# A hybrid of scan, linear attention and routed attention: image passes whose step and input rows are copied by DMA from SBUF rows

## The chip, the cores and the metric
The kernel runs on one core of one Trainium2 chip. The metric is device time in microseconds of one launch. All work is in float32, but for the three bfloat16 parts into which the kernel before splits the scan's rows.

## The reference, cut to what matters
The input is four images of 16 x 16 places with 192 channels. One layer follows another:

```
x = x + conv_scan(group_norm(x))     # per image: in_proj to 96 + 96, 3x3 depthwise conv, silu,
                                     # 4 selective scans over 256 places, layer norm, gate, out_proj
t = t + performer(layer_norm(t))     # 12 heads of 16, 64 features: relu(.) + 0.001
t = t + ffn_attn(layer_norm(t))      # router picks 6 of 12 heads, softmax attention, layer norm
# one scan direction k (rows, columns, and both backwards), 96 channels, 16 states per channel:
d = softplus(dt_proj(x_dbl) + b);  h = h * exp(d * A) + (d * u) * B;  y = sum_n h * C
```

A scan has 96 x 16 = 1,536 independent recurrences for each image and direction, each 256 places long. `exp(d*A)` is called the decay, `d*u` the input, `(d*u)*B` the drive.

## The kernel before, in words
**Units.** The scans are done in units of 128 partitions x 512 elements. A unit holds 8 channels x 16 states on its partitions and two images of 256 places side by side in its row. There are 2 halves of two images x 4 directions = 8 scans, each of 12 units, so 96 units. Backward directions use inputs that GpSimd has laid out in reverse (`orders`, L516 to L530).

**One unit.** The step `d` and the input `d*u` are made once for each scan on 96 partitions, one for each channel (`step2`, L976 to L997). A unit needs each channel row on 16 partitions. The row is split into bfloat16 parts hi, mid and lo (ScalarE L720 and L724, GpSimd L544 and L549), which DMAs on SyncE's queue stack above one another (L446), and TensorE spreads them with a 0/1 matrix into PSUM: `step_bc` (L1384) and `inp_bc` (L1388), each with two banks. ScalarE makes the decay from `step_bc` (L732, `decay`). VectorE multiplies `inp_bc` by the rows of B (L1010) and runs the recurrence (L1019, `state`). GpSimd multiplies `state` by the rows of C (L559, `outp`), and TensorE sums the 16 states with a 0/1 band into `y_acc` (L1397), a float32 matmul that shows as two. The rows of B and C lie on 32 partitions in `bc`, and eight DMAs each copy 16 of these partitions to the 128 partitions of `b_rep` and `c_rep` (L433).

**Order.** Each engine has one instruction stream, written out by hand: a loop over 96 units, and after it the list `rest`. Semaphores join the streams. Between two units stand items from the planner `side_work`: the making of the next scan's rows (`preparing`, with fixed places such as PRE_RAW and PRE_INP), the second half's convolution, the transposes of weights, and from unit 52 on the attention and feed-forward steps of images 0 and 1 (`ATTN_STEPS`, `FFN_STEPS`), one or two steps a unit. Images 2 and 3 can start only when unit 95 is done, because a scan holds two images. The planner, run on its own constants, leaves 91 steps in `rest`: the end of image 0 from its second head step (`t0`), image 1 from `hT`, and all of images 2 and 3. A step's vector part stands in `side` of each engine: VectorE adds the 0.001 and takes the maximum for the queries (L1161) and the keys (L1166), and applies the norms (L1062).

**SyncE's queue** holds all DMAs in one order: the loads, then for each scan eight copies of B, eight of C, and nine of the stack.

Of the kernel before, what the change touches and what calls it, by code (L numbers as in the profile page):

```python
# [24 lines left out]
P = 128  # L25
IMAGES, SIDE, CH = 4, 16, 192
L = SIDE * SIDE
HALVES = 2
IMG = IMAGES // HALVES
TOK = IMG * L  # L30
TILES = TOK // P
CK = CH // 2
DI, NS, RANK, DIRS = 96, 16, 12, 4
GRP = P // NS
UNITS = DI // GRP
CHUNK = 32
CHUNKS = DI // CHUNK
PER_CHUNK = CHUNK // GRP
# [7 lines left out]
RING = 3  # L46
SLOTS = 3
STATE_SLOTS = 4
Y_LAG = 3
# [6 lines left out]
PRE_RAW, PRE_CLIP, PRE_EXP, PRE_SERIES, PRE_LN = -4, -3, -2, -1, -1  # L56
PRE_MAX, PRE_MAX_SERIES, PRE_INP = 0, 1, 2

PRE_HI, PRE_REST, PRE_MID, PRE_LO = (2, 3), (4, 5), (5, 6), (6, 6)
SECOND_LATER = 3  # L60
LOG_MAX = 82.0

CONST2 = 3 + 1 + HPC + TOPK
ONES = 13
BEHIND = (0, 0, 0, 6)
FIRST_STEP = 4
ADD_Y = 3
Z_GATED = 2
ACC_ROWS = IMG * (SIDE + 2) - 2
SCANS = HALVES * DIRS  # L70
# [6 lines left out]
HEAD_STEPS = ["s0", "t0", "s1", "w0", "t1", "w1"]  # L77
# [9 lines left out]
FRONT_BESIDE = ((1, "xh"), (9, "conv0"), (11, "conv1"), (13, "conv2"), (17, "silu"), (21, "z"))  # L87
WEIGHTS_FIRST = 14

UNITS_AFTER = {step: 1 for step in ("q0", "q1", "q2", "kv00", "kv01", "kv10", "wqk", "wv", "fq", "fk")}  # L90
# [4 lines left out]
def side_work():  # L95

    beside = [[] for _ in range(SLOT_COUNT)]

    for at, step in FRONT_BESIDE:
        beside[at].append((step, 1))  # L100
    for i, step in enumerate(WEIGHT_STEPS):
        beside[WEIGHTS_FIRST + 2 * i].append((step, 0))
# [3 lines left out]
    done, ready = [0, 0], [DIRS * UNITS + FIRST_STEP, DIRS * UNITS + FIRST_STEP + 1]  # L106
    for u in range(DIRS * UNITS, SLOT_COUNT):
        held = 0.0
        for n in (0, 1):
            if ready[n] > u or done[n] >= (len(steps) if n == 0 else done[0]):  # L110
                continue
            step = steps[done[n]]
            if step in HEAD_STEPS and (n % IMG or step == "w0"):
# [8 lines left out]
    at = {step: i for i, step in enumerate(steps)}  # L122
    done += [0, 0]
    rest = []
    while min(done) < len(steps):
        for n in range(IMAGES):
            if done[n] == len(steps) or (n and done[n - 1] < min(len(steps), done[n] + 1 + BEHIND[n])):
                continue
            if n >= IMG and (done[n] == at["tT"] and done[n - IMG] <= at["fv"] or done[n] == at["un"] and done[n - IMG] <= at["fo"]):
                continue  # L130
            rest.append((steps[done[n]], n))
            done[n] += 1
# [3 lines left out]
def products(step, n):  # L136
# [7 lines left out]
    if step in HEAD_STEPS:  # L144
        heads = range(int(step[1]), TOPK, 2)
        return {"s": [f"s{n}{j}" for j in heads], "t": [f"pt{n}{j}" for j in heads], "w": [f"pv{n}", f"pd{n}"] * (step == "w0")}[step[0]]
# [3 lines left out]
def preparing(u, at):  # L150

    n = (u - at) // UNITS + 1
    if u == max(0, at + SECOND_LATER - (at > PRE_INP)):
# [4 lines left out]
def ring_plan():  # L158

    beside, rest = side_work()  # L160
    names = ["w_in", "gm0", "w_xp", "w_dt", "gv0", "w_alog", "xh0_0", "xh1_0", "w_fold", "gm1", "z_0", "gv1", "d0"]
# [9 lines left out]
    for i, name in enumerate(names):  # L171
        if name[:2] in ("pv", "pd"):
            at = FINAL_RING - 2 + (name[1] == "d")
        else:
            at = turn % (RING if i < early else FINAL_RING - 2)
            turn = turn + 1 if i + 1 != early else 0
# [5 lines left out]
def hybrid_kernel(nc, x, in_proj_w, conv_w, conv_b, x_proj_w, dt_w, dt_b, A_logs, Ds, norm_g, norm_b, out_proj_w,  # L182
# [5 lines left out]
    with ExitStack() as ctx:  # L188
# [31 lines left out]

        step_bc = [ctx.enter_context(nc.psum_tensor(f"step_bc{i}", [P, TOK], F32)) for i in range(2)]
        inp_bc = [ctx.enter_context(nc.psum_tensor(f"inp_bc{i}", [P, TOK], F32)) for i in range(2)]
        y_acc = ctx.enter_context(nc.psum_tensor("y_acc", [P, TOK], F32))
        banks = [ctx.enter_context(nc.psum_tensor(f"ring{i}", [P, TOK], F32)) for i in range(RING)]
        banks += step_bc + inp_bc + [y_acc]

        def bank(name):
# [3 lines left out]
        x_tok = sb("x_tok", [P, HALVES * TILES, CH])  # L231
# [11 lines left out]
        band = sb("band", [P, 2 * DI - GRP])  # L243
        spread = sb("spread", [DI, PER_CHUNK, P], BF16)
# [17 lines left out]
            "room_b", [([CK, 2, HALVES * TOK], F32), ([FEAT, HPC, FEAT], F32), ([FEAT, HPC, HD], F32), ([CK, HPC, FEAT], F32)],  # L262
            [([P, PAIRS, TOK], F32)])
        valr = sb("valr", [1, IMG, 3 * HEADS, HD])
        acc, opw, hn = shared("room_e", [([DI, ACC_ROWS, SIDE], F32), ([CK, 2, DI], F32)], [([P, TILES, CH], F32)])
# [19 lines left out]
        xpad, wsel1 = shared("room_w", [([DI, IMG, SIDE + 2, SIDE + 2], F32)], [([CK + 1, 2, 3, CK], F32)])  # L285
# [1369 lines left out]
```

## Time and profile before

| | us |
|---|---|
| median of 3 runs (lowest, highest) | 463.25 (460.02, 463.73) |
| profiled execution: its own time | 463.01 |
| its span, first to last instruction | 461.3 |
| busy of the span: TensorE matmul, VectorE, ScalarE, GpSimd | 371.3, 346.4, 179.8, 206.9 |
| moved by DMA | 12.69 MB |

The profile is of one execution. Busy time of an engine counts its compute instructions alone. PE is TensorE's matmul, PEld its weight load, DVE VectorE, ACT ScalarE, POOL GpSimd, SPq SyncE's queue. The granted clock is TensorE's, as a share of full speed. The DMA share is the mean busy share of the core's 16 DMA engines. In a row, "idle before" is time in which the engine had nothing running just before such an instruction, and the name behind it is what ended that time.

### The profile page before, as it was taken

The numbers are of one execution on the slowest core, as the hardware profiler recorded it, in microseconds if no ns is written. First come the engines' busy times: TensorE is split into PE (matmuls) and PEld (weight loads), VectorE is DVE, ScalarE is ACT, GpSimd is POOL, SyncE is SP. The second block draws the span as 40 slices with busy tenths as digits, with TensorE's granted clock in tenths as the row PEclk, the third lists the DMA queues.
The fourth block names the chain that finished last, engine by engine and source line by source line (L and its number), as shares of the span: only waits on it lengthen the run. The fifth ranks groups of instructions, "written<-read, shape, count | busy, mean of one in ns | idle before, by whom it ended". The sixth has DMA issues, their size and how long they took to land. (4 is left out here: it accounts for less than half of the span.)

```text
span 461.3 us, 5553 instructions
## 1 busy us (share of the span) xinstructions
PE 371.3 (80%) x1669; PEld 214.3 (46%) x1669; DVE 346.4 (75%) x622; ACT 179.8 (39%) x405; POOL 206.9 (45%) x210
## 2 busy tenths in 40 slices
PE   5825499697887867857999998896989999969691
PEld 4612133142332312323557555553865786958450
DVE  5885989878999999999789898987457356263514
ACT  2565354554563534423243332335225211135340
POOL 7131697867895967774653863451121010000001
PEclk9999889979897987785999999999799989588966
DMA  5502212011121110110101010000000000000000
GB/s 121 106 21 64 56 26 64 23 41 34 23 58 34 47 40 18 40 43 9 47 21 33 11 34 1 0 2 1 2 17 1 1 0 17 2 1 1 1 17 18
DMA packets 15743, 12.69 MB, mean 28 GB/s; under 512 B 7279, under 2 KB 11361, under 8 KB 15713
## 3 DMA queue, kind: packets, MB, share of 16 engines
q1 hardware_dynamic: 15713, 12.33, 11.7%
q8 instruction: 14, 0.23, 0.2%
q14 instruction: 16, 0.13, 0.1%
HBM read 2.62 MB, written 0.79 MB: 7 GB/s over the span
## 5 line engine op out<-in xcount | busy, mean ns | idle before, releaser
L559 POOL TENSOR_TENSOR outp<-state,c_rep 128x512 f32<-128x512 f32 x96 | 126.4, 1321 | 93.0 <-PE y_acc L1397 43.1
L1019 DVE TENSOR_TENSOR_SCAN state<-decay,inp_bc 128x512 f32<-128x512 f32 x96 | 117.2, 1221 | 9.3 <-DVE inp_bc L1010 4.3
L1397 PE MATMUL y_acc<-outp,band 128*96 128x512 f32 x192 | 111.2, 666 | 6.7 <-DVE y_sum L1034 2.6
L732 ACT ACTIVATE decay<-step_bc,a_neg 128x510 f32<-128x510 f32 x96 | 64.9, 683 | 47.0 <-PE step_bc L1384 46.8
L1010 DVE TENSOR_TENSOR inp_bc<-b_rep,inp_bc 128x512 f32<-128x512 f32 x96 | 65.5, 682 | 7.1 <-PE inp_bc L1388 6.9
L1388 PE MATMUL inp_bc<-room_s,spread 96*128 96x512 bf16 x96 | 41.0, 427 | 31.1 <-DVE state L1019 31.0
L494 POOL TENSOR_TENSOR rs<-mv,neg_half 128x2 f32<-128x2 f32 x16 | 11.1, 696 | 120.0 <-DVE mv L1055 119.9
L1384 PE MATMUL step_bc<-room_s,spread 96*128 96x512 bf16 x96 | 39.9, 415 | 12.7 <-DMA room_s<-lo 11.6
L1397 PEld LDWEIGHTS y_acc<-outp,band 128*96 128x96 f32 x192 | 34.3, 182 | 24.7 <-issue 10.3
L1388 PEld LDWEIGHTS inp_bc<-room_s,spread 96*128 96x128 bf16 x96 | 9.9, 103 | 65.9 <-DVE state L1019 56.8
L1384 PEld LDWEIGHTS step_bc<-room_s,spread 96*128 96x128 bf16 x96 | 10.4, 109 | 32.5 <-issue 27.3
L720 ACT CAST hi<-step 96x512 bf16<-96x512 f32 x16 | 9.9, 616 | 33.4 <-DVE step L989 24.7
L1507 PE MATMUL ring<-kvw,tT 96*128 96x480 f32 (+1 forms) x48 | 21.2, 567 | 0.0
L1132 DVE RECIPROCAL spl<-y_acc 96x256 f32<-96x256 f32 x4 | 7.0, 1754 | 15.4 <-PE y_acc L1436 15.4
L1125 DVE TENSOR_REDUCE nmax<-ring 128x2 f32<-128x512 f32 x19 | 12.0, 680 | 7.1 <-PE step_bc L1407 3.9
L1501 PE MATMUL ring<-tT,qw 96*128 96x256 f32 (+1 forms) x64 | 16.6, 404 | 0.8 <-issue 0.8
L544 POOL TENSOR_TENSOR step<-step,hi 96x512 f32<-96x512 f32 x14 | 16.1, 1151 | 0.0
L549 POOL TENSOR_TENSOR lo<-step,mid 96x512 bf16<-96x512 f32 x14 | 15.9, 1154 | 0.0
L1501 PEld LDWEIGHTS ring<-tT,qw 96*128 96x128 f32 (+1 forms) x64 | 12.8, 202 | 5.9 <-issue 4.3
L724 ACT CAST mid<-step 96x512 bf16<-96x512 f32 x16 | 9.9, 616 | 13.6 <-POOL step L544 13.4
L1525 PEld LDWEIGHTS ring<-cbd,room_b 128*128 128x128 f32 x96 | 13.7, 227 | 1.0 <-issue 1.0
L1525 PE MATMUL ring<-cbd,room_b 128*128 128x34 f32 x96 | 13.6, 307 | 0.0
(346 smaller groups left out, 650.8 us busy)
## 6 DMA issues: line engine op xcount, KB each, us to landing
b_rep<-bc SPq DMA_DIRECT2D x64, 32.0 KB, 1.9
c_rep<-bc SPq DMA_DIRECT2D x64, 32.0 KB, 2.0
room_s<-hi SPq DMA_DIRECT2D x24, 64.0 KB, 2.0
room_s<-mid SPq DMA_DIRECT2D x24, 64.0 KB, 2.0
room_s<-lo SPq DMA_DIRECT2D x24, 64.0 KB, 2.0
x_tok<-in_x_dram SPq DMA_DIRECT2D x2, 384.0 KB, 3.8
out_dram<-room_g SPq DMA_DIRECT2D x4, 192.0 KB, 2.0
room_a<-in_L_attn_w_qkv_dram SPq DMA_DIRECT2D x1, 432.0 KB, 6.5
```

Source lines behind the costliest of these rows:

```text
L544: g.tensor_tensor(step2[:, i, :], step2[:, i, :], hi[:, i, :], ALU.subtract).then_inc(S["rest"], 1)
L549: g.tensor_tensor(lo[:, i, :], step2[:, i, :], mid[:, i, :], ALU.subtract).then_inc(S["lo"], 1)
L559: g.tensor_tensor(outp[:, u % SLOTS, :], state[:, u % STATE_SLOTS, :], c_rep[:, n % 2, :], ALU.mult).then_inc(S["outp"], 1)
L732: a.activation(decay[:, u % SLOTS, :, 1:L], step_bc[u % 2][:, :].rearrange("p (b l) -> p b l", b=IMG)[:, :, 1:L], ACT.Exp, scale=a_neg[:, ...
L1010: v.tensor_tensor(inp_bc[u % 2][:, :], b_rep[:, n % 2, :], inp_bc[u % 2][:, :], ALU.mult).then_inc(S["drive"], 1)
L1019: v.tensor_tensor_scan(state[:, u % STATE_SLOTS, :], decay[:, u % SLOTS, :, :].rearrange("p b l -> p (b l)"), inp_bc[u % 2][:, :], 0.0, AL ...
L1384: t_.matmul(step_bc[u % 2][:, :], spread[:, q, :], stack[:, n % 2, j, 0:TOK], start=True, stop=True).then_inc(S["bc_step"], 1)
L1388: t_.matmul(inp_bc[u % 2][:, :], spread[:, q, :], stack[:, n % 2, j, TOK:2 * TOK], start=True, stop=True).then_inc(S["bc_inp"], 1)
L1397: t_.matmul(y_acc[0:DI, :], band[:, at:at + DI], outp[:, u % SLOTS, :], start=(g12 == 0), stop=(g12 == UNITS - 1)).then_inc(S["y_mm"], 1)
L1501: ins = t_.matmul(b_[:, u * L:(u + 1) * L], qw[0:CK + c, c, i * P:(i + 1) * P], tT[0:CK + c, c, at0:at0 + L], start=(c == 0), stop=(c == 1))
L1507: ins = t_.matmul(b_[:, 0:w], tT[0:CK + c, c, at:at + P], kvw[0:CK + c, c, j, :], start=(c == 0), stop=(c == 1))
L1525: ins = t_.matmul(b_[:, at:at + w], qp[:, i, at0 + t * P:at0 + (t + 1) * P], cbd[:, b, i, :], start=True, stop=True)
```

## The change: what it does
**Units are cut another way.** A unit is now 16 channels x 8 states of one image; its row holds two ways through the image, row order and column order. A scan is one image in one direction (forward or back): 4 images x 2 = 8 scans of 12 units, again 96. Backward scans read the same rows with a reversed access pattern, so two of three reordered copies go.

**How rows reach 128 partitions.** The bfloat16 split, the stack and the spreading matmuls go. For each unit one DMA on SyncE's queue reads 16 rows of `step2` (step and input side by side, 4 KB a partition) eight times over and writes 128 partitions of `in_rep` (512 KB). `in_rep` has four slots; the DMA of unit u + 4 waits for the decay and the drive of unit u. `step2` has two homes, so one scan's rows are made while the other's are read. B is spread by TensorE with replicated weights into two PSUM banks, `b_bc`, once for each scan and half of the states (`fill_b`). The rows of C go to DRAM and come back as two 256 KB broadcasts a scan.

**Engines.** ScalarE's decay reads SBUF and takes two instructions a unit, one for each way. VectorE keeps the product with B and the scan; the product goes to one bank, `drv`, and waits for the scan before it. `pre_inp` moves to GpSimd. The additions of 0.001 and of epsilon move to GpSimd, the relu of queries and keys and the norms `tn` and `un` to ScalarE. `y_acc` is summed in three bands of 32 rows, three units at a time.

**Order.** The planner works on all four images: image 0's attention starts at unit 28, image 1's at 52, image 2's at 78, and `rest` holds 64 steps: image 1 from `t0`, image 2 from `q2`, and all of image 3. At the start only image 0 is convolved ahead of the first unit; the others' input projections (`inner`) stand before the first `d` product in TensorE's stream.

```diff
-GRP = P // NS
+SN = 8
+GRP = P // SN
+IN_SLOTS = 4
-PRE_RAW, PRE_CLIP, PRE_EXP, PRE_SERIES, PRE_LN = -4, -3, -2, -1, -1
+PRE_RAW, PRE_CLIP, PRE_EXP, PRE_SERIES, PRE_LN = 0, 1, 2, 3, 3
...
+        b_bc = [ctx.enter_context(nc.psum_tensor(f"b_bc{i}", [P, TOK], F32)) for i in range(PARTS)]
+        drv = ctx.enter_context(nc.psum_tensor("drv", [P, TOK], F32))
+        in_rep = sb("in_rep", [P, IN_SLOTS, 2, TOK])
+        step2 = sb("step2", [DI + NS, 2, 2, TOK])
...
+        def unit(u):
+            n, g = u // UNITS, u % UNITS
+            third, q = g % GROUPS % CHUNKS, g % GROUPS // CHUNKS
+            return n // PER_IMAGE, n % PER_IMAGE, g // GROUPS, PER_CHUNK * third + q
...
+            def repeat_c(n, i):
+                sp.wait_ge(S["c_kept"], 16 * (n + 1))
+                if n:
+                    sp.wait_ge(S["outp"], UNITS * (n - 1) + GROUPS * (i + 1))
+                sp.dma_start(c_rep[:, i, :], c_rows[n % 2, i].unsqueeze(0).to_broadcast([GRP, SN, TOK])).then_inc(S["c_there"][i], 16)
+
+            def repeat_step(u):
+                _, _, _, g = unit(u)
+                n = u // UNITS
+                if u % UNITS == 0:
+                    sp.wait_ge(S["step"], n + 1)
+                if u >= IN_SLOTS:
+                    sp.wait_ge(S["decay"], u - IN_SLOTS + 1)
+                    sp.wait_ge(S["drive"], u - IN_SLOTS + 1)
+                rows = step2[GRP * g:GRP * (g + 1), n % 2, :, :].rearrange("p a t -> p (a t)")
+                sp.dma_start(in_rep[:, u % IN_SLOTS, :, :].rearrange("p a t -> p (a t)"),
+                             rows.unsqueeze(1).to_broadcast([GRP, SN, 2 * TOK])).then_inc(S["in_there"][u % IN_SLOTS], 16)
...
-                a.activation(decay[:, u % SLOTS, :, 1:L],
-                             step_bc[u % 2][:, :].rearrange("p (b l) -> p b l", b=IMG)[:, :, 1:L],
-                             ACT.Exp, scale=a_neg[:, at:at + 1]).then_inc(S["decay"], 1)
+                for e in range(WAYS):
+                    at = (part * DIRS + WAYS * back + e) * GROUPS + c16
+                    ins = a.activation(decay[:, back, u % DECAY_SLOTS, e, kept],
+                                       in_rep[:, slot, 0, :].rearrange("p (e l) -> p e l", e=WAYS)[:, e, kept],
+                                       ACT.Exp, scale=a_neg[:, at:at + 1])
+                ins.then_inc(S["decay"], 1)
...
-                v.tensor_tensor(inp_bc[u % 2][:, :], b_rep[:, n % 2, :], inp_bc[u % 2][:, :],
-                                ALU.mult).then_inc(S["drive"], 1)
+                if u:
+                    dve.wait_ge(S["state"], u)
+                v.tensor_tensor(drv[:, :], in_rep[:, slot, 1, :], b_bc[part][:, :], ALU.mult).then_inc(S["drive"], 1)
...
+            def fill_b(n, part):
+                if n:
+                    pe.wait_ge(S["drive"], UNITS * (n - 1) + GROUPS * (part + 1))
+                for e in range(WAYS):
+                    k = WAYS * (n % PER_IMAGE) + e
+                    ins = t_.matmul(b_bc[part][:, e * L:(e + 1) * L], w_b[:, k, part, :], xs[:, i, e, :], start=True, stop=True)
...
-                t_.matmul(y_acc[0:DI, :], band[:, at:at + DI], outp[:, u % SLOTS, :],
+                    t_.matmul(y_acc[rows, :], band[:, at:at + CHUNK], outp[:, u % SLOTS, :],
```

## Rows read from the trace of the kernel before

**Rows 1.** Stages: length, busy us of PE, PEld, DVE, ACT, POOL; clock, DMA share, GB/s.
```profile
41.00:311.00 270.00, 226.26 (x772) 106.01 (x771) 243.76 (x334) 112.64 (x214) 178.81 (x150) 0.90 0.14 32
311.00:461.30 150.30, 124.32 (x822) 93.34 (x820) 73.45 (x210) 47.15 (x147) 13.52 (x18) 0.85 0.02 6
```
**Rows 2.** Groups of the unit loop: shapes xcount | busy us, mean ns | idle before.
```profile
L559 POOL TENSOR_TENSOR outp<-state,c_rep 128x512 f32<-128x512 f32 x96 | 126.4, 1321 | 93.0 <-PE y_acc L1397 43.1 <-DVE state L1019 36.5 <-DMA c_rep<-bc 13.1
L1019 DVE TENSOR_TENSOR_SCAN state<-decay,inp_bc 128x512 f32<-128x512 f32 x96 | 117.2, 1221 | 9.3 <-DVE inp_bc L1010 4.3 <-ACT decay L732 2.0
L1397 PE MATMUL y_acc<-outp,band 128*96 128x512 f32 x192 | 111.2, 666 | 6.7 <-DVE y_sum L1034 2.6 <-POOL outp L559 2.3 <-DVE y_sum L1037 1.8
L732 ACT ACTIVATE decay<-step_bc,a_neg 128x510 f32<-128x510 f32 x96 | 64.9, 683 | 47.0 <-PE step_bc L1384 46.8
L1388 PE MATMUL inp_bc<-room_s,spread 96*128 96x512 bf16 x96 | 41.0, 427 | 31.1 <-DVE state L1019 31.0
L1384 PE MATMUL step_bc<-room_s,spread 96*128 96x512 bf16 x96 | 39.9, 415 | 12.7 <-DMA room_s<-lo 11.6 <-ACT fv L606 0.9
```
**Rows 3.** VectorE's groups in the stage 41 to 311 us.
```profile
L1010 DVE TENSOR_TENSOR inp_bc<-b_rep,inp_bc 128x512 f32<-128x512 f32 x95 | 64.8, 682 | 3.9 <-PE inp_bc L1388 3.7
L997 DVE TENSOR_TENSOR step<-step,room_g 96x512 f32<-96x512 f32 x7 | 4.7, 678 | 0.0
L1166 DVE TENSOR_SCALAR room_a<-ring 128x384 f32<-128x384 f32 x8 | 4.4, 552 | 1.9 <-PE ring L1507 1.6
L1161 DVE TENSOR_SCALAR room_b<-ring 128x512 f32<-128x512 f32 x6 | 4.1, 687 | 2.1 <-PE ring L1501 2.1
L1044 DVE TENSOR_TENSOR y_sum<-y_sum,y_acc 96x256 f32<-96x256 f32 x6 | 3.2, 581 | 0.5 <-PE y_acc L1397 0.5
L1062 DVE TENSOR_SCALAR room_h<-x_tok,mv,rs 128x192 f32<-128x192 f32 x4 | 3.2, 845 | 0.0
L1062 DVE TENSOR_SCALAR room_e<-x_tok,mv,rs 128x192 f32<-128x192 f32 x2 | 0.6, 364 | 0.0
L1055 DVE TENSOR_SCALAR mv<-mv 128x2 f32<-128x2 f32 x6 | 2.4, 402 | 0.2
```
**Rows 4.** Groups of the whole span for what moves or comes.
```profile
L755 ACT ACTIVATE room_s<-ring,nmax 128x256 f32<-128x256 f32 x20 | 7.7, 481 | 10.8 <-DVE nmax L1125 10.8
L720 ACT CAST hi<-step 96x512 bf16<-96x512 f32 x16 | 9.9, 616 | 33.4 <-DVE step L989 24.7 <-DVE step L997 8.6
L544 POOL TENSOR_TENSOR step<-step,hi 96x512 f32<-96x512 f32 x14 | 16.1, 1151 | 0.0
L1125 DVE TENSOR_REDUCE nmax<-ring 128x2 f32<-128x512 f32 x19 | 12.0, 680 | 7.1 <-PE step_bc L1407 3.9 <-PE ring L1407 3.2
L1132 DVE RECIPROCAL spl<-y_acc 96x256 f32<-96x256 f32 x4 | 7.0, 1754 | 15.4 <-PE y_acc L1436 15.4
```
**Rows 5.** Start of the first scan, in order of time (start us, us); VectorE.
```profile
20.39 4.10 DVE L958 SCALAR_TENSOR_TENSOR room_e<-room_w,cw,room_e 96x256 f32<-96x256 f32 x8
33.66 0.69 DVE L997 TENSOR_TENSOR step<-step,room_g 96x512 f32<-96x512 f32 x1
```
**Rows 6.** Start, in order of time; ScalarE and SyncE's queue.
```profile
30.59 1.92 ACT L618 ACTIVATE room_b<-inp_bc,gbi,grs 96x256 f32<-96x256 f32 x4
28.91 4.99 SPq L433 DMA_DIRECT2D b_rep<-bc  x8
```
**Rows 7.** Three stretches by DMA: input load, one b_rep copy, one hi copy (columns as 1).
```profile
2.50:4.50 2.00, 0.22 (x2) 0.24 (x2) 1.56 (x4) 0.00 (x0) 1.87 (x5) 1.00 1.07 357
30.14:30.54 0.40, 0.00 (x0) 0.00 (x0) 0.40 (x1) 0.40 (x1) 0.40 (x2) 1.00 0.37 82
36.18:36.63 0.45, 0.00 (x0) 0.00 (x0) 0.42 (x2) 0.45 (x2) 0.00 (x0) 1.00 0.60 146
```
**Rows 8.** DMA from 30.1 to 35 us in 40 slices, eight b_rep copies: GB/s; then the issues.
```profile
GB/s 117 84 67 0 0 84 100 67 17 0 67 117 50 34 0 50 117 67 34 0 50 100 84 34 0 0 150 67 50 0 0 134 67 67 0 0 100 84 84 0
b_rep<-bc SPq DMA_DIRECT2D x64, 32.0 KB, 1.9
```

More of the change, by code:

```diff
@@ L126, in side_work @@
         for n in range(IMAGES):
[L127 to L132, printed above, removed]
+            if may_go(n):
+                rest.append((steps[done[n]], n))
+                done[n] += 1
     return beside, rest
@@ L171, in ring_plan @@
     for i, name in enumerate(names):
[L172 to L176, printed above, removed]
+        at = turn % (RING if i < early else FINAL_RING)
+        turn = turn + 1 if i + 1 != early else 0
         plan[name] = (i, at, held[at])
@@ L676, in weights @@
+            for n in range(1, IMAGES):
+                group_normed(n)
+            for n in range(1, IMAGES):
+                pad(n)
             def weights(step):
@@ L913, in _ @@
+            group_bias(0, one)
+            turned_stats(2, 1)
+            for c in range(2):
+                turned_stats(3, c)
+            collected(1, IMAGES, 2 * IMAGES)
             for e in range(2):
@@ L1046, in statistics @@
-            def statistics(n, i, src_of, tag, eps):
+                back = unit(u)[1]
+                order = slice(None, None, -1) if back else slice(None)
+                held = decay[:, back, u % DECAY_SLOTS, :, :].rearrange("p e l -> p (e l)")
+                v.tensor_tensor_scan(state[:, u % STATE_SLOTS, :][:, order], held[:, order], drv[:, :][:, order],
+                                     0.0, ALU.mult, ALU.add).then_inc(S["state"], 1)
+            def add_y(n):
+                b = n % IMG
+                dve.wait_ge(S["y_mm"], PER_IMAGE * UNITS * (n + 1))
+                if n == 0:
+                    dve.wait_ge(S["small"], 1)
+                if n >= IMG:
+                    fetched(dve, f"yT_{n - IMG}")
+                v.scalar_tensor_tensor(y_sum[:, b, :], xs[:, n, 0, :], dsum[:, 0:1], y_acc[0:DI, 0:L],
+                                       ALU.mult, ALU.add).then_inc(S["y_part"], 1)
+                dve.wait_ge(S["y_part"], n + 1)
+                turned = y_sum[:, b, :].rearrange("p (y x) -> p x y", x=SIDE)
+                v.tensor_tensor(turned, turned, y_acc[0:DI, L:2 * L].rearrange("p (x y) -> p x y", x=SIDE),
+                                ALU.add).then_inc(S["y_ev"], 1)
@@ new lines, in sum_states @@
+            def sum_states(first):
+                g = first % (PER_IMAGE * UNITS)
+                n = first // (PER_IMAGE * UNITS)
+                pe.wait_ge(S["outp"], first + BATCH)
+                if g == 0 and n > 0:
+                    pe.wait_ge(S["y_ev"], n)
+                for u in range(first, first + BATCH):
+                    c16 = unit(u)[3]
+                    rows = slice(CHUNK * (c16 // PER_CHUNK), CHUNK * (c16 // PER_CHUNK + 1))
+                    at = CHUNK - GRP - GRP * (c16 % PER_CHUNK)
+                    t_.matmul(y_acc[rows, :], band[:, at:at + CHUNK], outp[:, u % SLOTS, :],
+                              start=(g == 0), stop=(g == PER_IMAGE * UNITS - BATCH)).then_inc(S["y_mm"], 1)
@@ L1595, in side @@
                     done(ins)
-            front("z", 0)
+            for n in range(1, IMAGES):
+                inner(n)
             b_ = begin("d0")
```

937 lines of the change are left out of this document (423 added, 514 removed).

## The prediction
> **What bounds the kernel now.** I read the busy shares by stage first. The unit loop runs from 41 to 311 us, and what is left of the attention steps takes the last 150.3 us [rows 1]. In the loop VectorE is busy 243.8 of 270 us and TensorE 226.3; in the tail TensorE leads with 124.3 of 150.3. Then the groups of the unit loop: VectorE spends 0.682 + 1.221 = 1.90 us on a unit and hardly idles before either [rows 2, 3], while GpSimd idles 93.0 us before its product, for TensorE's `y_acc` and for the scan in turn, and ScalarE 47.0 us before the decay, for the spread rows. TensorE in its turn waited 31.0 us for the scan before it could refill `inp_bc`. So the loop is a ring of VectorE and TensorE, VectorE ahead, and 270 / 96 = 2.81 us a unit is 1.90 of unit work, 0.64 of other VectorE work and 0.27 of idling. DMA is far from a bound: a mean share of 0.14 in this stage.
>
> **VectorE's part.** Product and scan keep their shapes, so 1.90 us a unit stays. What leaves VectorE in the loop: seven `pre_inp` (L997) 4.7 us, keys 4.4, queries 4.1, norms 3.8, epsilon 2.4, and of the adding of `y_acc` half of L1044's 3.2 and about as much of its two other forms [rows 3]: 22 us. What comes in, because three images now run beside the loop: image 0 from its second head step, image 1 up to its first, and image 2 up to `q1`. From the maxima of 0.68 and the reciprocal of 1.75 [rows 4] and the like I count 7.5 + 7.5 + 4, 19 us. VectorE would be busy some 240 us in the loop: lighter a step, not lighter in all. With TensorE out of its way, idling falls from 26 us to about 22: 262 us if nothing else bounds. The single `drv` bank costs nothing beyond that, since VectorE runs product and scan in order anyway; its price is a semaphore turn of at most the 0.1 us a unit that L1019 idles now (9.3 us for 96), and that is inside the 22.
>
> **TensorE, ScalarE, GpSimd.** TensorE loses 39.9 + 41.0 us of spreading [rows 2] and gains 64 passes of 256 columns for B, which at the 0.67 us of a 512-column pass of `y_acc` are at most 43 us. ScalarE loses the casts (28 of 0.616 in the loop, 17 us) and pays two decays of at most 0.48 us in place of 0.683 [rows 2, 4], 27 us more, plus relu and norms: some 145 of 262 us. GpSimd loses 28 subtractions of 1.15, 32 us, and gains seven products of such a size (8 us) and thirteen additions of at most that (15 us) [rows 4]. None of the three reaches VectorE's 240, so I cost these edits at nothing. That cover is good: without it the added work on ScalarE would be those 27 us.
>
> **The DMA.** This is the new resource. SyncE's issue costs 4.99 / 8 = 0.62 us [rows 6], and with 96 + 8 x 3 issues that is 75 us over the loop: hidden. The transfer is not small: a unit takes 128 x 4 KB = 524,288 bytes, 50 MB in all, against 12.69 MB in the kernel before. The trace shows no such transfer, so I bound it. The input load, from DRAM to 128 partitions, moves 357 GB/s [rows 7]: 1.5 us a unit. One b_rep copy reads 16 SBUF partitions, as the new ones do; it moves 82 GB/s at a share of 0.37, and 82 / 0.37 = 222 GB/s with all engines busy would be 2.4 us. But this divides by busy time, and busy time grows when engines wait for each other in a packet: the same quotient is 357 / 1.07 = 334 for the input load, and 146 / 0.60 = 243 for the hi copy from 32 partitions. Something slows the packets of copies whose source and target are few partitions. The slices of the eight b_rep copies peak at 117 GB/s three times, with one of 134 and one of 150 [rows 8]. If 16 source partitions can't give more than 117, a unit takes 4.5 us; the slowest reading, 82 GB/s over the whole copy, would be 6.4, but there the engines start one after another, which a queue four units deep hides. So the bounds are 1.5 and 4.5. The nearest row is the copy with the same 16 source partitions, which gives 2.4 and 4.5, midway 3.4. I take 3.3, a little below, because successive units read other partitions, up to four are queued, and an engine that is ahead can go on to them.
>
> **The sum, against the profiled execution's 463.0.** Start: the convolution of the second image goes (4.1 + 0.4 us, [rows 5]), but ahead of the first product now stand the norms of three images (6 of 0.48, 2.9 us) [rows 6] and the padding of these images, and the product waits for one reordering; these cancel. The rows are ready at 34.4 us as now [rows 5]. Issue and the way to the first packet are 30.14 - 28.91 = 1.2 us [rows 6, 7]: packets flow from 35.6. Then 96 x 3.3 = 316.8 us. The sixteen broadcasts of C, 256 KB each, go through the same DMA engines: at 357 GB/s 0.73 us each, 11.8. From the last landing to the last scan 0.5 + 0.9 + 1.2 = 2.6. The loop ends at 366.8. The tail holds 64 steps where it held 91: 150.3 x 64 / 91 = 105.7. Counting TensorE's work instead gives about the same (image 1's end 17, image 2's rest 32, image 3's 39, so 88 of the 124 us). Sum 472.5, and 463.0 - 461.3 = 1.7 around the span: **474, predicted 475**, 2.6% above the median of 463.25, from which the profiled execution hardly differs. From the start the loop would cost 96 x 0.49 us more a unit than now, and the shorter tail gives back 45 us.
>
> **Rival 1: the copies hide.** If all engines stay busy on different partitions (1.5 to 2.4 us), the DMA is under VectorE's 2.7 a unit. The first scan comes at 39, the loop takes 262, the tail 105.7, and 1.7: **408**, with 398 to 430 for the idling. For it: 222 GB/s is what the share says, and four slots give 8 us of lead. Against it: no slice with SBUF sources holds such a rate. It decides below 2.7 us a unit.
>
> **Rival 2: the sixteen rows are the bound, strictly.** All engines of a unit read the same 16 partitions, four engines to four neighbours, and if they stay in step nothing of the next unit helps. At 117 GB/s: 35.6 + 96 x 4.5 + 11.8 + 2.6 + 105.7 + 1.7 = **589**. For it: packets were slow just where partitions were few. Against it: those copies were single, with a ramp each.
> By the Trainium skill, page "SBUF — State Buffer", section "Door 1: The DMA port swizzle", DMA rate depends on how many of 16 ports the partitions reach, and partitions 0 to 15 reach four and measured 104 GB/s. By that figure a unit would be an estimated 5.0 us and the kernel about 640. The trace's 82 to 150 GB/s agree with it so far as single copies can, but it has no sustained stream; nor does the page say that reading the same rows again is bound like writing.
>
> **Rival 3: the tail doesn't shrink.** With images 2 and 3 no longer equal, the last image's chain may bound it: 120 in place of 105.7 adds 14 to any case. It is in the ranges.
>
> **How the numbers follow.** About 1%, 4.6 us, is what a measurement can tell here: the runs shown lie between 460.0 and 463.7. My forecast, 2.9 to 4.0 us a unit, is 436 to 541 and gets 0.43; rival 1 gets 0.32, rival 2 and what lies above my forecast 0.25. The range must take in most of rival 1 and reach rival 2: 404 to 590 leaves out some 0.10 below and 0.08 above. Faster by over 1% is below 458.6: rival 1 and the part of the forecast under 3.13 us a unit (0.09), 0.41. Within 1% is 0.07 of the forecast. Slower is the rest, 0.52.
>
> **What would show it.** In the profile after, look first at the windows of the loop: a DMA share near 1 at 140 to 180 GB/s, with VectorE idle before the product for `in_rep`, is my forecast; 105 to 120 GB/s is rival 2; a share well under 1, with VectorE over 90% busy, rival 1. The time from a copy's issue to its landing tells the same: near 2 to 4 us if hidden, over 8 if four are queued up. The first scan should start at 39 to 42 us, and the loop's end to the span's end should be 100 to 120 us with TensorE leading. I am wrong as a whole if a semaphore wait that I cost at nothing holds SyncE's queue: the wait for C's old rows (`outp`) stands ahead of the next unit's copy, and would show as idle time before SyncE's issue ended by `outp`.

## The result and the profile after

The changed kernel takes **596.33 us** (median of 4 runs, 593.1 to 600.1) against 462.47 us of the kernel before on the same chip (4 runs, 460.02 to 463.73): ratio 1.291, 95% interval [1.280, 1.301]. That is 121 us above my 475 and outside the range. Where the runs of a kernel below fall into two groups, up to 2% apart, kernels are compared by the quicker group.

Stages of the profile after, the same columns as [rows 1]: the unit loop, from the first scan to the last, and the tail.

```profile
44.90:454.30 409.40, 228.39 (x858) 132.51 (x858) 241.18 (x349) 146.68 (x367) 181.44 (x166) 0.62 0.90 133
454.30:598.30 144.00, 115.44 (x637) 87.31 (x634) 45.28 (x125) 44.05 (x127) 29.72 (x38) 0.75 0.02 5
```

VectorE is busy 241.18 us in the loop, where I counted 240. New in that row are its 168 us of idling, a DMA share of 0.90 and 133 GB/s, and a granted clock of 0.62 for 0.90; TensorE and GpSimd are as busy as before. 96 scans start between 44.9 and 453.1 us, 4.30 us a unit. The tail is 144 us where I had 105.7.

The groups of the unit loop, to be held against [rows 2, 3]:

```profile
L569 POOL TENSOR_TENSOR outp<-state,c_rep 128x512 f32<-128x512 f32 x96 | 126.0, 1315 | 170.1 <-DVE state L1019 115.6
L742 ACT ACTIVATE decay<-in_rep,a_neg 128x255 f32<-128x255 f32 x192 | 86.8, 500 | 244.9 <-DMA in_rep<-step 244.8
L1008 DVE TENSOR_TENSOR drv<-in_rep,b_bc 128x512 f32<-128x512 f32 x96 | 66.5, 693 | 135.0 <-DMA in_rep<-step 133.0
L1019 DVE TENSOR_TENSOR_SCAN state<-decay,drv 128x512 f32<-128x512 f32 x96 | 117.2, 1221 | 30.7 <-ACT decay L742 26.8
L1367 PE MATMUL y_acc<-outp,band 128*32 128x512 f32 x192 | 56.4, 974 | 87.0 <-POOL outp L569 81.0
```

Product and scan cost what they did, and both readers of `in_rep` wait for its copy: ScalarE 244.8 us, VectorE 133.0. The chain of waits on the page of the profile, as shares of the span, says it in one line:

```profile
DMA in_rep<-step 57%; SPq L446 4%; SPq L458 2%; PE b_bc L1486 2%; PE drv L1497 2%; PE ring L1389 2%; PE ring L1472 1%; PE ring L1250 1%; PE ring L1478 1%; POOL room_a L594 1%; ACT decay L742 1%; PE ring L1486 1%; PE ring L1534 1%; PE y_acc L1405 1%; DMA room_h<-in_L_conv_in_proj_w_dram 1%
```

The DMA issues (count, KB each, us to landing), and then how long SyncE was in one issue of them (min/median/max ns):

```profile
in_rep<-step SPq DMA_DIRECT2D x96, 512.0 KB, 11.8
c_rep<-c_rows SPq DMA_DIRECT2D x16, 256.0 KB, 10.0
```
```profile
L458 SPq DMA_DIRECT2D in_rep<-step x96: 544/3772/4719, 36.5 to 439.9; - x96
```

A copy lands 11.8 us after its issue begins, which is 2.7 units of 4.30 us. So between two and three copies were under way, not four. The issue itself, 0.54 us when the queue is free, takes 3.8 us in the median. The sign that I had set for being wrong as a whole, SyncE waiting for `outp`, is absent: where SyncE waited in the loop, it was nearly always for ScalarE's decay to free a slot (146.2 us, 65 times).

### The profile page after: what moved, and what is told of

It is laid out like the page before. It is cut to its first block, busy times and chain, and to the rows that moved or that the text cites. A ratio compares the mean times of both kernels' runs of the same rounds, so it can differ in the third digit from the quotient of the medians.

```text
span 598.3 us, 5534 instructions
## 1 busy us (share of the span) xinstructions
PE 368.1 (62%) x1595; PEld 238.4 (40%) x1595; DVE 305.7 (51%) x539; ACT 207.0 (35%) x533; POOL 221.4 (37%) x241
## 4 chain that ended last, share of the span: by engine, by line
DMA 57%; PE 21%; SPq 7%; DVE 6%; issue 3%; POOL 3%; ACT 3%; POOLq 0%; ACTq 0%; DVEq 0%
DMA in_rep<-step 57%; SPq L446 4%; SPq L458 2%; PE b_bc L1486 2%; PE drv L1497 2%; PE ring L1389 2%; PE ring L1472 1%; PE ring L1250 1%; PE ring L1478 1%; POOL room_a L594 1%; ACT decay L742 1%; PE ring L1486 1%; PE ring L1534 1%; PE y_acc L1405 1%; DMA room_h<-in_L_conv_in_proj_w_dram 1%
## 5 line engine op out<-in xcount | busy, mean ns | idle before, releaser
L742 ACT ACTIVATE decay<-in_rep,a_neg 128x255 f32<-128x255 f32 x192 | 86.8, 500 | 244.9 <-DMA in_rep<-step 244.8
L1008 DVE TENSOR_TENSOR drv<-in_rep,b_bc 128x512 f32<-128x512 f32 x96 | 66.5, 693 | 135.0 <-DMA in_rep<-step 133.0
L1019 DVE TENSOR_TENSOR_SCAN state<-decay,drv 128x512 f32<-128x512 f32 x96 | 117.2, 1221 | 30.7 <-ACT decay L742 26.8
L1367 PE MATMUL y_acc<-outp,band 128*32 128x512 f32 x192 | 56.4, 974 | 87.0 <-POOL outp L569 81.0
L590 POOL TENSOR_SCALAR room_b<-room_b 128x512 f32<-128x512 f32 x12 | 18.8, 1565 | 36.8 <-ACT room_b L786 36.8
L594 POOL TENSOR_SCALAR room_a<-room_a 128x384 f32<-128x384 f32 x16 | 19.0, 1186 | 23.1 <-ACT v L804 23.0
L1353 PE MATMUL b_bc<-xs,w_b 96*128 96x256 f32 x64 | 24.7, 529 | 0.0
L1428 PE MATMUL ring<-room_c 96*96 96x256 f32 x54 | 19.6, 526 | 6.8 <-ACT outT L628 6.8
L1353 PEld LDWEIGHTS b_bc<-xs,w_b 96*128 96x128 f32 x64 | 16.4, 270 | 7.6 <-issue 3.3
L1389 PE MATMUL ring<-ident,prob 128*128 128x128 f32 x76 | 14.8, 355 | 2.6 <-DVE y_sum L1034 1.3
## 6 DMA issues: line engine op xcount, KB each, us to landing
in_rep<-step SPq DMA_DIRECT2D x96, 512.0 KB, 11.8
room_h<-in_L_conv_in_proj_w_dram SPq DMA_DIRECT2D x1, 144.0 KB, 4.4
room_a<-in_L_attn_w_proj_dram SPq DMA_DIRECT2D x1, 144.0 KB, 5.2
```

The lines of the kernel that those rows point to most:

```text
L742: ins = a.activation(decay[:, back, u % DECAY_SLOTS, e, kept], in_rep[:, slot, 0, :].rearrange("p (e l) -> p e l", e=WAYS)[:, e, kept], AC ...
L1008: v.tensor_tensor(drv[:, :], in_rep[:, slot, 1, :], b_bc[part][:, :], ALU.mult).then_inc(S["drive"], 1)
L1019: v.tensor_tensor_scan(state[:, u % STATE_SLOTS, :][:, order], held[:, order], drv[:, :][:, order], 0.0, ALU.mult, ALU.add).then_inc(S["st ...
L1353: ins = t_.matmul(b_bc[part][:, e * L:(e + 1) * L], w_b[:, k, part, :], xs[:, i, e, :], start=True, stop=True)
L1367: t_.matmul(y_acc[rows, :], band[:, at:at + CHUNK], outp[:, u % SLOTS, :], start=(g == 0), stop=(g == PER_IMAGE * UNITS - BATCH)).then_inc ...
L1389: ins = t_.transpose(b_[:, (2 * kt + q) * P:(2 * kt + q + 1) * P], prob[:, j // 2, q, kt * P:(kt + 1) * P], idn)
```

## Experiments on the copies

Theory A: a copy is bound by the few source partitions that it reads. The expectations name its rivals. "Loop" below is from the first scan's start to the last's; the stage rows run on to its end, some 1.2 us more.

**The same rows from DRAM.** One more DMA a scan (384 KB) keeps the rows in DRAM first, and the 96 copies of the same 512 KB read them there. Nothing else changes.

```diff
+def keep_rows(n):
+    sp.wait_ge(S["step"], n + 1)
+    sp.dma_start(d_rows[n % 2], step2[0:DI, n % 2, :, :] ...)
-rows = step2[GRP * g:GRP * (g + 1), n % 2, :, :] ...
+rows = d_rows[n % 2, GRP * g:GRP * (g + 1), :]
```

> The step and input rows of each scan go to DRAM first (one copy of 384 KB a scan), and each unit's 512 KB are read from there, to the same 128 partitions, with the same number of issues. Theory A (the 16 source partitions bound the copy): the reading is off SBUF, a unit's transfer takes 1.5 to 2 us and hides; the loop falls from 4.3 us a unit to VectorE's 2.5 to 2.8, about 240 to 270 us, and the kernel to 420 to 450 us. Theory B (the 128 target partitions, or the bytes as such, bound it): no change, 590 to 600. Theory C (SyncE's issue or its waits bound it): no change either, since issues and waits stay, perhaps 5 us more for the way through DRAM.

Measured: 483.69 us, ratio to before 1.048 [1.043, 1.054]. Two stretches of its loop, then loop and tail, and a copy's landing:

```profile
46.00:66.00 20.00, 7.01 (x28) 3.87 (x28) 17.41 (x22) 13.67 (x35) 13.70 (x11) 0.50 1.03 240
66.00:120.00 54.00, 38.59 (x147) 19.99 (x144) 49.42 (x61) 32.98 (x80) 35.18 (x29) 0.78 1.02 251
```
```profile
45.90:341.00 295.10, 197.69 (x862) 122.66 (x863) 248.17 (x350) 145.54 (x367) 180.18 (x167) 0.71 0.76 193
341.00:480.00 139.00, 110.57 (x632) 85.01 (x630) 44.98 (x124) 43.99 (x127) 29.59 (x38) 0.76 0.02 5
```
```profile
in_rep<-d_rows SPq DMA_DIRECT2D x96, 512.0 KB, 5.6
```

The same bytes to the same 128 partitions by the same queue go at 240 to 251 GB/s with the DMA engines full in these stretches (a share of 1.02 and 1.03), 2.1 to 2.2 us a unit for the 1.5 to 2 that I expected, and the loop is 3.1 us a unit. So neither the volume, nor the writing, nor the queue held the changed kernel at 133.

**Every sixth partition.** The source stays in SBUF, but a unit's 16 channels are taken from every sixth partition, and `y_acc` is one band of 96 rows again to match.

```diff
-rows = step2[GRP * g:GRP * (g + 1), n % 2, :, :] ...
+rows = step2[g:DI:GROUPS, n % 2, :, :] ...
```

> A unit takes every sixth channel instead of 16 neighbours, so its 16 source rows lie spread over the 96 partitions; bytes, issues and targets are the same, and the state sum goes back to 96 columns for each unit. Theory A: neighbours no longer share a way out, at most two of the 16 rows do, so a unit's copy falls from 4.3 us to under 2.6, the loop is VectorE's, and the kernel takes 430 to 470 us (TensorE's sums are longer again). Theories B and C: 590 to 600 us.

Measured: 483.83 us, ratio 1.047 [1.042, 1.052]; the loop runs from 43.2 to 341.4.

```profile
43.20:342.60 299.40, 230.22 (x846) 130.87 (x846) 243.65 (x349) 144.92 (x367) 180.89 (x166) 0.83 0.70 181
```
```profile
in_rep<-step SPq DMA_DIRECT2D x96, 512.0 KB, 4.7
```

Sixteen partitions as before, only farther apart, and the copy no longer holds the loop: theory A, and what counted was not how many partitions are read but where they lie. In the trace's records of single packets, one of 4 KB took 0.47 us on average in the changed kernel and 0.26 us here.

**Another order of blocks.** Sixteen neighbours again, but successive units read blocks 0, 1, 4, 2, 3, 5 of the 96 partitions in place of 0, 2, 4, 1, 3, 5.

```diff
-third, q = g % GROUPS % CHUNKS, g % GROUPS // CHUNKS
-return ..., PER_CHUNK * third + q
+return ..., BLOCKS[g % GROUPS]       # (0, 1, 4, 2, 3, 5)
```

> Only the order of the six groups of 16 channels is changed, so that no two units in a row read rows of the same partitions modulo 32 (blocks 0, 1, 4, 2, 3, 5 for 0, 2, 4, 1, 3, 5). Theory A with engines that stay in step: no change, 590 to 600. Theory A with engines that run ahead into the next unit's copy (what my forecast of 3.3 us assumed): the next unit now always reads by another way, so 3.0 to 3.8 us a unit and 480 to 550 us. Theories B and C: no change.

Measured: 541.05 and 550.44 us (2 runs). The profile is of the longer one; its loop runs from 45.5 to 405.1, 3.8 us a unit.

```profile
45.50:406.30 360.80, 237.54 (x855) 123.57 (x858) 248.69 (x349) 146.02 (x367) 179.87 (x166) 0.72 0.87 151
```

So engines that are ahead do go on to the next unit's rows, and where those rows lie decides what that gives: 151 GB/s in this order, 133 in the changed kernel's. By the Trainium skill, page "SBUF — State Buffer", section "Door 1: The DMA port swizzle", partitions 0 to 31 share their ports with partitions 32 to 63, and those from 64 on lie on other ports. By that the changed kernel's order reads blocks 0 and 2, and blocks 1 and 3, one after the other from the same ports, and no two successive blocks of the other order share theirs. The runs agree with that. (The expectation's "modulo 32" isn't quite it: blocks 4 and 2, and 3 and 5, are successive there and equal modulo 32.)

**Two input slots.**

```diff
-IN_SLOTS = 4
+IN_SLOTS = 2
```

> The changed kernel itself with two input slots in place of four. My forecast of 3.3 us a unit rested on up to four queued copies, with engines that run ahead into the next unit. If a queue of four is what lets 16 source partitions give 133 GB/s (3.9 us for a unit at full rate) where the single copies before peaked at 117, two slots lose some of it: 4.5 us a unit or more, 96 x 0.2 = 20 us or more above 596: 615 to 640. If SyncE's issue holds the queue at two copies anyway, as its 3 us an issue suggest, it changes only what stands behind the wait for ScalarE's decay: 596 to 605.

Measured: 642.18 us, loop 45.6 to 497.7, 4.76 us a unit, landing 8.3 us.

```profile
45.60:498.90 453.30, 228.20 (x862) 132.66 (x863) 241.98 (x350) 146.69 (x367) 181.26 (x166) 0.61 0.91 120
```

Four slots are worth 0.46 us a unit over two: the lead that I counted on exists and is small. The total is just above the 615 to 640 of that branch, and the other, 596 to 605, is out.

**Half the bytes.** Only the step row is copied, 256 KB a unit; VectorE's product reads it too, so the scan's input isn't the reference's.

```diff
-rows = step2[GRP * g:GRP * (g + 1), n % 2, :, :]    # 4 KB a row
+rows = step2[GRP * g:GRP * (g + 1), n % 2, 0, :]    # 2 KB a row
```

> Only the step row of each unit is copied (2 KB a partition, 256 KB a unit), and VectorE's product reads it in place of the input row, so the scans' input is not the reference's. Theory A and B: the transfer halves to about 2.15 us a unit, the loop becomes VectorE's at 2.5 to 2.8, the kernel takes 430 to 460 us. Theory C: the same number of issues with the same waits, near 590 us.

Measured: 480.35 us (one run). From the same 16 neighbours, half the bytes hide: a loop of 296 us with as many issues. That speaks against C, and does not separate A from B.

## Experiments on the loop and the tail

With the copies hidden three ways the kernel still takes 480 to 484 us, where rival 1 had 408 and the three expectations 420 to 470. Loop and tail each miss by some 33 us. I first took the waits between engines for the cause.

**Queries and keys on VectorE** (theory D), on the kernel with rows from DRAM, as are all that follow unless it is said. One instruction does relu and addition, as in the kernel before.

```diff
-a.activation(qp[...], bank(name), ACT.Relu)                    # ScalarE
-g.tensor_scalar(qp[...], qp[...], KERNEL_EPS, None, ALU.add)   # GpSimd
+v.tensor_scalar(qp[...], bank(name), KERNEL_EPS, KERNEL_EPS, ALU.add, ALU.max)
```

> As the kernel with rows read from DRAM (483.7 us; loop 295.1 us with VectorE idle for 47, tail 139.0), but the queries' and keys' 0.001 and maximum are made by VectorE in one instruction, as in the kernel before: GpSimd's 28 additions (1.19 to 1.57 us each, 37.8 us in all) and ScalarE's relus go, and VectorE gets 28 instructions of 0.55 to 0.69 us, some 17 us, 10 of them in the loop. Theory D, the chain relu, addition, cx/at product across three engines is what holds the steps up: VectorE's idle time in the loop falls from 47 to about 25 us, which pays for the added 10, so the loop is 280 to 287, and the tail loses about one addition of 1.2 to 1.6 us behind each key and query group, 139 to some 128 to 132: 460 to 470 in all. Theory E, ScalarE has too short a lead: idle stays near 40, the loop is 297 to 305, the tail 135: 480 to 490. Theory F, TensorE's lower granted clock and its instruction count set both: loop 300, tail 139: 484 to 492.

Measured: 476.51 us, the median of 471.05, 472.65, 480.37 and 480.62. The profile is of the quickest.

```profile
45.00:339.30 294.30, 200.49 (x862) 122.39 (x863) 249.87 (x365) 139.03 (x352) 162.15 (x151) 0.71 0.77 193
339.30:469.00 129.70, 102.26 (x632) 76.17 (x630) 51.46 (x138) 38.01 (x114) 12.59 (x25) 0.82 0.02 5
```

By the quicker two, 471.9, that is 12 us less than with rows from DRAM alone, and the loop is as long as before: VectorE is idle for 44 us in it, not for 25. The tail is 9 us shorter, but at a granted clock of 0.82 for 0.76, so D's own share isn't separated there.

**A longer lead for ScalarE** (theory E), and **both edits**:

```diff
-IN_SLOTS, DECAY_SLOTS = 4, 2
+IN_SLOTS, DECAY_SLOTS = 3, 3
```

> As the kernel with rows read from DRAM, with three decay slots a direction in place of two and three input slots in place of four: ScalarE may be three units ahead of the scan. Theory E, the long gaps of VectorE (7.5, 4.0, 6.2, 3.2 us, behind a decay that stands in ScalarE's stream behind a side step that waits) come from the short lead: one more unit of lead, some 2.8 us for each of about six gaps, gives back 10 to 15 us of the loop's 295 and nothing of the tail: 469 to 475. Theory D: the gaps are longer than one unit and most stay, 479 to 484. Theory F: 484. If three input slots are too few for the copy (5.6 us from issue to landing, under two units), the time goes up to 490.

> Both edits, VectorE makes queries and keys and three decay slots, on the kernel with rows read from DRAM. If D and E each are half of it, their gains add: loop 275 to 282, tail 128 to 132, 455 to 463, at or just under the kernel before (462). If both have the same cause (a waiting side step in ScalarE's stream), the second adds under 5 us to the better one. Theory F: 484 to 490.

Measured: 488.26 us (1.056 [1.053, 1.059]) for the lead alone. For both, 481.46, and 477.7 by the two quicker of four runs (1.034 [1.029, 1.039]). Each is 5 to 6 us slower than without the lead. This doesn't refute E, since the edit also took an input slot away: ScalarE's wait for the copies doubled, as the expectation had feared. First without the lead, then with it:

```profile
L750 ACT ACTIVATE decay<-in_rep,a_neg 128x255 f32<-128x255 f32 x192 | 86.5, 503 | 66.4 <-DMA in_rep<-d_rows 36.4
L750 ACT ACTIVATE decay<-in_rep,a_neg 128x255 f32<-128x255 f32 x192 | 86.3, 503 | 74.6 <-DMA in_rep<-d_rows 74.4
```

Whether a longer lead with four input slots would pay stays open. The gain from queries and keys on VectorE comes again, 11 us (488.3 to 477.7).

**On the kernel with every sixth partition**, both edits:

> The same two edits on the kernel that reads every sixth partition of the SBUF rows (483.8 us, first scan 43.2). Its loop was bound like the other's at 3.1 us a unit with the copies hidden (DMA share 0.70), so theory D and E give the same loop as in the kernel with both edits, and the start is 2.7 us earlier: 452 to 461. If the copies from SBUF bound it (share over 0.85 once the loop is quicker), it ends 5 to 15 us above that kernel.

Measured: 479.22 us (1.034 [1.027, 1.041]), above what was expected. Its loop is 296.9 us at a granted clock of 0.81; with rows from DRAM and both edits it was 299.0 at 0.68.

**What the wait looks like.** Lines of the kernel with queries and keys on VectorE, in order of time (start us, us):

```profile
172.81 1.22 DVE L1014 TENSOR_TENSOR_SCAN state<-decay,drv 128x512 f32<-128x512 f32 x1 [3.98 <-ACT decay L742]
173.04 5.33 PE L1503 MATMUL ring<-cbd,room_b 128*128 128x34 f32 x24
178.41 0.31 DVE L1145 RECIPROCAL arec<-ring 128x24 f32<-128x24 f32 x1 [4.38 <-PE ring L1503]
180.01 1.22 DVE L1014 TENSOR_TENSOR_SCAN state<-decay,drv 128x512 f32<-128x512 f32 x1
```

VectorE's stream has a step of the attention between two units; its 24 matmuls run at a granted clock of 0.50, the 1.2 GHz level, in 5.33 us, and the next scan stands 7 us behind the last. In the kernel before, the same 24 took 2.77 us at 1.00, and 2.76 in its loop:

```profile
371.47 2.77 PE L1525 MATMUL ring<-cbd,room_b 128*128 128x34 f32 x24
```

So either TensorE's clock is at fault (theory G) or the order of the steps, which leaves too little time between product and reader (theory H).

**TensorE kept busy in the loop:** pairs of matmuls with zero weights.

```diff
+for _ in range(2):
+    t_.matmul(y_acc[0:CHUNK, :], none[0:DI, :], xs[:, 0, ...], start=False, stop=False)
```

> The kernel with rows read from DRAM and queries and keys on VectorE (476.5 us; loop 293 us at a granted clock of 0.71, TensorE busy 199; tail 131), with two more matmuls into y_acc in two of three units, 112 in all, with weights of zero, so that sums don't change. They are 112 x 0.59 = 66 us more work for TensorE. Theory G, TensorE's low granted clock makes the small products of cx and at (24 matmuls in 5.3 us against 2.6 to 2.8 where it was at the high level) longer than the one unit that is left for them, and VectorE waits: the clock in the loop rises to 0.85 to 1, the waits for at's product (7.6 us) and most of the decay's (9.8) and others go, the loop is 275 to 282 in spite of the added work: 458 to 466 us. Theory H, the gaps come from the order of the steps alone: the clock may rise, but the added matmuls stand ahead of products in TensorE's stream, the loop is 293 to 305: 476 to 490.

Measured: 500.34 us (1.085 [1.079, 1.090]).

```profile
L1606 PE MATMUL y_acc<-xs,none 96*32 96x512 f32 x220 | 123.2, 692 | 1.5 <-ACT fv L630 1.5
```
```profile
45.80:363.70 317.90, 275.54 (x1061) 123.78 (x1062) 249.95 (x364) 138.14 (x352) 162.03 (x151) 0.85 0.71 179
```

A poor test. I had priced a matmul from 56.4 us over 96, but those go in threes, each into another band of 32 rows, and three take 1.93 us together even at a granted clock of 0.50 (the row below); the added ones, two into the same band, cost 1.1 us each, 123.2 in all, and stood in front of the products.

```profile
171.18 1.93 PE L1372 MATMUL y_acc<-outp,band 128*32 128x512 f32 x6
```

The clock rose to 0.85 and the loop grew by 24 us. What the clock alone costs in the loop stays open. The kernel with every sixth partition doesn't tell either: its loop had a clock of 0.83 for the 0.71 with rows from DRAM and was as long, but TensorE was busy for 230 us in it, not for 198.

**The plan's spacing.** Two units behind eight kinds of step that the change had set to one, as in the kernel before.

```diff
-UNITS_AFTER = {... "gT", "tT", "kv11", "cx", "aT", "hT", "fv", "t0" ...: 1}
+UNITS_AFTER = {...}      # these eight: 2
```

> The same kernel (rows from DRAM, queries and keys on VectorE, 476.5 us), with the planner's gaps as in the kernel before: two units, not one, behind gT, tT, kv11, cx, aT, hT, fv and t0. Five more steps fall into the tail (69 for 64), some 8 to 10 us. Theory H: the products that are waited for (at 7.6 us, ScalarE's decay behind cx and kv) are there in time, VectorE's idle time falls from 44 to about 25 and the loop from 293 to 272 to 278, so 463 to 470. Theory G: the products are slow on a cold TensorE however they are spaced, but spacing helps there too by half: 475 to 482. If the loop gives nothing back, 485.

Measured: 476.93 us (1.035 [1.030, 1.041]).

```profile
45.50:322.00 276.50, 195.62 (x805) 113.16 (x806) 247.31 (x356) 136.27 (x337) 162.82 (x151) 0.70 0.82 206
322.00:473.00 151.00, 122.89 (x688) 89.24 (x688) 53.71 (x146) 40.75 (x129) 12.91 (x25) 0.73 0.02 5
```

The loop is as H said: 18 us shorter at the same clock, idling of VectorE down from 44 to 29. But it also holds five steps fewer, and no run separates their going from the spacing. The total is 5 us above the 471.9 of the quicker runs without this edit, since the tail takes the five steps and 21 us. On the whole the edit moved work across the border and gained nothing.

**Image 3's tail steps left out.** The tail holds 31 steps for 64; image 3's output is not its own.

```diff
-while min(done) < len(steps): for n in range(IMAGES): ...
+while min(done[:3]) < len(steps): for n in range(3): ...
```

> The kernel with rows from DRAM and queries and keys on VectorE (tail 131 us, profiled time 471), with image 3's 33 attention and feed-forward steps left out; its output is another image's rows. The tail then holds image 1's last 6 steps and image 2's last 25, alone: nothing stands between two dependent steps. Chain theory: the tail is one image's chain of dependent steps through TensorE, ScalarE, VectorE and GpSimd, and the other image's steps hide in its gaps: 25 of 33 steps alone take nearly the same, 25/33 x 131 = 95 to 105 us, 440 in all. Work theory: TensorE's work sets it, and half the steps take half, 31/64 x 131 = 60 to 70 us: 405 in all.

Measured: 437.38 us (one run).

```profile
45.30:338.90 293.60, 198.87 (x861) 122.77 (x862) 249.68 (x365) 139.15 (x352) 162.12 (x151) 0.70 0.77 194
338.90:435.70 96.80, 63.70 (x353) 45.34 (x351) 29.07 (x72) 22.14 (x64) 6.46 (x11) 0.68 0.02 7
```

With 353 of 632 of TensorE's instructions the tail still takes 96.8 of 129.7 us, and TensorE is busy 63.7 of them, at a granted clock of 0.68 for 0.82, so a small part of that length is the clock's. The tail is in the chain theory's range of 95 to 105 and far from the other's 60 to 70: an image's steps depend on one another. Image 2's 25 steps are the longest chain here, 3.9 us a step. At that pace image 3's 33 steps would take an estimated 128 us, about the 129.7 of the whole tail. By this estimate the 64-step list is as long as its longest chain, one whole image.

**TensorE kept busy in the tail:**

```diff
+for _ in range(2):      # behind each tail step
+    t_.matmul(y_acc[0:CHUNK, 0:P], none[:, :], ident[:, :], start=True, stop=True)
```

> The same kernel (476.5 us, tail 131 at a granted clock of 0.82 in its profiled run) with two small matmuls with weights of zero behind each of the 64 tail steps, into the bank of y_acc, which leaves the final ring (seven banks): 128 columns, two records each of 0.2 to 0.4 us, 128 such matmuls. Clock theory: TensorE idles less, the granted clock in the tail rises to 0.9 or more, and the products' gain pays for the added 27 us or more: tail 125 to 135, 470 to 478. If the clock isn't what costs, the added matmuls stand ahead of the chain: tail 150 to 165, 495 to 510.

Measured: 489.01 us (1.058 [1.053, 1.064]).

```profile
343.40:489.70 146.30, 129.65 (x888) 89.62 (x886) 51.98 (x138) 38.13 (x114) 12.58 (x25) 0.92 0.02 5
```
```profile
L1609 PE MATMUL y_acc<-ident,none 128*32 128x128 f32 x256 | 41.0, 291 | 1.5 <-ACT fv L630 1.5
```

The added 41.0 us of TensorE's time lengthened the tail by only 17, and the granted clock is 0.92 for 0.82. The rest of TensorE's work took 88.6 us in place of 102.3. So TensorE's products ran faster at the higher clock. What that gave the tail isn't separated, since TensorE had 27 us of idle time there which the added matmuls could fill, and 146 us lies between the two ranges expected of the tail. This way of raising the clock costs more than it gives.

**The version that the findings point to:** every sixth partition, VectorE's queries and keys, the plan's old spacing.

> Every sixth partition read straight from SBUF, queries and keys on VectorE, and the kernel before's gaps in the plan: first scan at 41 to 43 (2.5 to 4 us earlier than from DRAM), loop 275 as with rows from DRAM and the same plan if the copies stay hidden, tail 148 to 152: 466 to 474. If the copies from SBUF bound the quicker loop (2.9 us a unit; DMA share was 0.70 at 3.1, so 0.76), up to 480.

Measured: 473.27 us, 1.023 [1.019, 1.027]: 21% under the changed kernel, and still 11 us behind the kernel before. Loop and tail by the stage rows:

```profile
42.00:320.60 278.60, 213.62 (x806) 119.18 (x806) 243.57 (x356) 135.58 (x337) 163.74 (x151) 0.86 0.77 194
320.60:471.80 151.20, 123.15 (x688) 89.00 (x688) 53.72 (x147) 40.74 (x129) 12.91 (x25) 0.74 0.01 5
```

It is inside the range expected, but no quicker than the quicker runs of the kernel with rows from DRAM and queries and keys on VectorE (471.9).

## Why the prediction was wrong

The sum's own span was 472.5 us and became 598.3. The loop's end moved from 366.8 to 454.3, 87.5 us, and the tail is 38.3 us longer.

**The start** (wrong by 2 us, then more): the rows were ready at 36.5, not 34.4, and the first scan stood at 44.9, not at 39 to 42, since no copy landed in less than 7.1 us.

**VectorE's part** (right): 241.18 us busy for 240.

**The DMA term** (wrong, and most of the miss): copies and C's broadcasts were to take 316.8 + 11.8 = 328.6 us and took 96 x 4.30 = 413. Split by bytes at the 133 GB/s of the stage, a unit is 3.94 us for my 3.3, 61 us over the loop, and a broadcast of C 1.97 us for my 0.73, 20 us for sixteen. The records of packets split it otherwise: those of 2 KB, nearly all C's, took 0.09 us each, about 12 us on each DMA engine in all, as priced, and those of the copies 0.47 us each, 359 us on each engine. How long a broadcast holds the copies up was not measured. The step that failed is "a little below, because successive units read other partitions, up to four are queued, and an engine that is ahead can go on to them". The bounds held, but the row to stay near was the upper one, the 117 GB/s of [rows 8]. The reason was real and mis-sized: four slots over two gave 0.46 us a unit, and another order of blocks would have given 0.5 more. My quotient of rate and busy share (222 GB/s) told nothing: after the change 133 / 0.90 is 148, so a high share went with slow packets and told of no rate to spare. The marks that I set were a share near 1 at 140 to 180 GB/s for my forecast and 105 to 120 for rival 2; what came lies between. By size rival 2's 589 is 1.2% from the 596, and its mechanism, the neighbouring rows, is the one that both source experiments showed, though not "strictly". That the size fits is luck: its copies and broadcasts, 443.8 us, are 31 too long, and its tail is 38 too short.
By the Trainium skill, page "SBUF — State Buffer", section "Door 1: The DMA port swizzle", the figure for partitions 0 to 15 was 104 GB/s. Here the stage moved 133 with four slots and 120 with two, C's broadcasts included, so the rule, that the rate depends on the ports reached, held for reading the same SBUF rows again and again, and the figure was too low.

**The edits on ScalarE and GpSimd, "I cost these edits at nothing"** (right while the copies bound, wrong otherwise): with the copies hidden, queries and keys back on VectorE gave 12 and 11 us in two pairs of kernels, by the quicker runs.

**Rival 1** (408, wrong even when its condition held): with copies hidden, 480 to 484 us. In the loop VectorE was busy 248 and idle 47 us, for 240 and 22. With the kernel before's spacing, and five steps fewer in it, the loop was 18 us shorter; what makes up the rest stays open.

**The tail** (wrong by 38 us): "150.3 x 64 / 91" takes a tail for a heap of work. The tail without image 3 showed that it is mostly a chain: half the steps take three quarters of the time. And the longest chain hardly changed: the kernel before's list held images 2 and 3 whole, 34 steps each, and the changed kernel's still holds image 3 whole, 33 steps. The change took 27 steps off the list and one off that chain; the time went from 150.3 to 144.0. The check that I made beside it, TensorE's 88 of 124 us, missed as well, since it ran 637 instructions, 0.77 of 822, at a granted clock of 0.75 for 0.85. Rival 3 named this cause, put it at 14 us, and gave it no case of its own.

## What to carry to other kernels

Before a copy that spreads few SBUF rows over all partitions replaces another way, ask where the source rows lie: sixteen neighbours gave 133 GB/s here, and the same copy was hidden when it read every sixth partition or went by DRAM. Where a trace has a slow row of the same shape, take the slow row, not a quotient by busy time. A list of steps behind the main loop isn't priced by its length: look for the longest chain of one item in it, and for what is left for another item to fill.

## What the runs showed of the hardware

- SyncE's issue of a 512 KB copy is 0.54 us at best and 3.8 us in the median of the changed kernel: with four slots part of the queueing is time in which SyncE is held in the issue. With two slots, at an even slower copy, the median is 0.545 us:

```profile
L458 SPq DMA_DIRECT2D in_rep<-step x96: 544/545/3437, 37.1 to 488.4; - x96
```

- The same batch of 24 small matmuls took 5.33 us at a granted clock of 0.50 and 2.77 at 1.00. A low clock in the loop, 0.62 on average in the changed kernel, didn't carry over into the tail: its first 28 us have 0.81 and 1.00, and the next 14 us, in which TensorE was busy for 12.9, have 0.54.

```profile
454.00:468.00 14.00, 12.64 (x60) 7.61 (x58) 6.26 (x15) 6.85 (x16) 5.20 (x5) 0.81 0.00 0
468.00:482.00 14.00, 11.74 (x78) 6.54 (x78) 5.74 (x16) 5.59 (x16) 6.58 (x11) 1.00 0.01 2
482.00:496.00 14.00, 12.91 (x57) 12.39 (x58) 2.49 (x7) 1.07 (x3) 1.95 (x2) 0.54 0.05 15
```

- GpSimd needed 1.57 us to add a constant to 128 x 512 float32 in SBUF (the row below, of the changed kernel); VectorE added and took the maximum from PSUM in 0.69 us [rows 3].

```profile
L590 POOL TENSOR_SCALAR room_b<-room_b 128x512 f32<-128x512 f32 x12 | 18.8, 1565 | 36.8 <-ACT room_b L786 36.8
```
